# The terms of three field groups: two matrix products a quad instead of three

## What is computed

```python
emb = embed_table[f_ix, x_idx]
lin1 = w1_table[f_ix, x_idx].sum(axis=1, keepdims=True) + w1_bias
s = emb.sum(axis=1)
fm = 0.5 * ((s * s).sum(-1) - (emb * emb).sum(axis=(1, 2)))[:, None]
h = emb.reshape(n, F * D)
h = relu(h @ mlp_w1 + mlp_b1)
h = relu(h @ mlp_w2 + mlp_b2)
mlp_out = h @ mlp_w3 + mlp_b3
x0 = emb.transpose(0, 2, 1)
last = x0
feats = []
for W in (cin_w0, cin_w1, cin_w2):
    last = einsum('ndl,ndf,klf->ndk', last, x0, W)
    feats.append(last)
cin_result = concatenate(feats, -1).sum(axis=1) @ lin_w + lin_b
return lin1 + fm + mlp_out + cin_result
```

## Time and profile before

| what | value |
|---|---|
| time, median of 3 (lowest, highest) | 494.3 us (493.42, 496.37) |
| the profiled execution: time, span | 494.42 us, 492.6 us |
| mean granted clock of PE | 0.989 |
| PE, DVE, ACT, POOL busy | 455.9, 413.2, 369.8, 343.7 us |
| gathers | 358, from 3.6 us to 454.8 us |
| first `main` of tile 0 | 63.22 us |

### The profile page before, as it was taken

The page is one execution under the profiler, slowest core; times in us unless marked ns, Lnnn a source line. Parts: engine busy times, 40 slices in busy tenths (PEclk is TensorE's granted clock), DMA queues, the critical chain, the costliest instruction groups (busy, mean ns, idle before and its releaser), DMA issues.

```text
span 492.6 us, 6838 instructions
## 1 busy us (share of the span) xinstructions
PE 455.9 (93%) x2179; PEld 385.8 (78%) x2179; DVE 413.2 (84%) x873; ACT 369.8 (75%) x726; POOL 343.7 (70%) x363
## 2 busy tenths in 40 slices
PE   0998986899999999999999999999999999999698
PEld 0995764788888888888888788888888888878476
DVE  6163369789999999999999999899999999989756
ACT  0163496488888888888888888888898888788684
POOL 5777777777777777777777777777777777777000
PEclk9999999799999999999999999999999999999989
DMA  8953695222222222222222222122222222222000
GB/s 164 216 159 29 110 205 146 7 8 9 7 8 8 7 9 7 9 8 9 7 8 7 8 8 8 7 8 8 8 8 8 7 9 7 8 8 9 1 0 2
DMA packets 21602, 15.64 MB, mean 32 GB/s; under 512 B 12786, under 2 KB 19903, under 8 KB 21439
## 3 DMA queue, kind: packets, MB, share of 16 engines
q0 software_dynamic: 11456, 3.14, 18.4%
q1 hardware_dynamic: 7106, 10.05, 8.4%
q10 hardware_dynamic: 3005, 2.01, 2.0%
HBM read 14.97 MB, written 0.21 MB: 31 GB/s over the span
## 4 chain that ended last, share of the span: by engine, by line
POOL 65%; issue 21%; PE 5%; ACT 5%; DVE 1%; DMA 1%; POOLq 0%; DVEq 0%
POOL emb L506 65%; ACT ps_s L605 2%; ACT z_hi L598 2%; PE ps_mlp L1152 1%; ACT z_hi L600 1%; PE ps_q L1107 1%; PE ps_y L1138 1%; PE ps_s L1094 1%; PE ps_q L1108 0%; PE ps_q L1109 0%; DVE z_lo L804 0%; DMA emb<-rows,idx_raw 0%; DMA idx_raw<-x_idx 0%; PE ps_y L1194 0%; PE ps_y L1193 0%
## 5 line engine op out<-in xcount | busy, mean ns | idle before, releaser
L506 POOL DMA_INDIRECT emb<-rows,idx_raw x358 | 343.3, 959 | 111.4 <-issue 108.9
L804 DVE TENSOR_TENSOR z_lo<-ps_s,z_hi 128x512 fp32r<-128x512 f32 (+1 forms) x192 | 131.1, 683 | 35.0 <-ACT ps_s L605 34.4
L598 ACT ACTIVATE z_hi<-ps_s 128x512 fp32r<-128x512 f32 (+1 forms) x192 | 114.1, 594 | 37.5 <-PE ps_s L1094 37.1
L605 ACT ACTIVATE ps_s<-ps_s 128x512 f32<-128x512 f32 (+1 forms) x192 | 113.3, 590 | 0.7
L1107 PE MATMUL ps_q<-z_lo,zw_hi 128*127 128x512 f32 (+1 forms) x192 | 79.6, 415 | 8.0 <-DVE z_lo L804 4.8
L1193 PE MATMUL ps_y<-look_hi,one_hot 128*128 128x442 f32 x232 | 85.0, 366 | 0.6 <-issue 0.4
L1094 PE MATMUL ps_s<-xt,pick 128*128 128x512 f32 (+1 forms) x192 | 77.1, 404 | 5.4 <-ACT x_two L591 4.9
L1194 PE MATMUL ps_y<-look_lo,one_hot 128*128 128x442 f32 x232 | 82.2, 356 | 0.0
L1109 PE MATMUL ps_q<-z_hi,zw_hi 128*127 128x512 f32 (+1 forms) x192 | 76.0, 396 | 0.0
L1108 PE MATMUL ps_q<-z_hi,zw_lo 128*127 128x512 f32 (+1 forms) x192 | 76.0, 396 | 0.0
L1107 PEld LDWEIGHTS ps_q<-z_lo,zw_hi 128*127 128x127 f32 (+1 forms) x192 | 36.5, 190 | 20.9 <-issue 11.0
(11 more groups left out here) (187 smaller groups left out, 686.7 us busy)
## 6 DMA issues: line engine op xcount, KB each, us to landing
emb<-rows,idx_raw POOLq DMA_INDIRECT x358, 3.0
w_space<-rows SPq DMA_DIRECT2D x2, 728.9 KB
m_space<-rows SPq DMA_DIRECT2D x2, 728.9 KB
w_space<-key_scratch SPq DMA_DIRECT2D x1, 1408.0 KB, 7.8
w<-cin_w SPq DMA_DIRECT2D x2, 416.0 KB, 5.9
w<-cin_w ACTq DMA_DIRECT2D x2, 416.0 KB, 9.0
w_space<-cin_w SPq DMA_DIRECT2D x2, 416.0 KB, 8.5
w_space<-cin_w ACTq DMA_DIRECT2D x2, 416.0 KB, 8.2
```

The costliest lines, as they stand in the source:

```text
L506: pool.indirect_dma_start(emb[t % EMB][:, f, :], None, rows, bass.IndirectOffsetOnAxis(row_ix[:, t, f:f + 1], 0)).then_inc(gathered[t] if ...
L598: act.activation(z_hi[0:k, c, :], ps[0:k, :], ACT.Square)
L605: act.activation(ps[0:k, :], ps[0:k, :], ACT.Square).then_inc(hi_ready, 1)
L804: z = dve.tensor_tensor(z_lo[0:k, u % NC, :], ps, z_hi[0:k, u % NC, :].bitcast(F32), ALU.subtract)
```

## The change

The three-group terms get by with two products a quad. One matrix `zt` holds both parts of the weights at different rows of the chunk. A triple (a, b, c) can be reached from the pair (a, c) with field b, or from the pair (b, c) with field a. The high part of its weight stands at the pair (a, c) and field b; the low part at the pair (b, c) and field a. Where the fields are 9, 16 and 17, the low part stands at the same pair, and at a second place of the field. For that `xt` now holds 30 places instead of 26: RUN = 10 fields from each of 0, 8 and 16 on (SHIFT = 8, RUNS = 3), so that fields 8, 9, 16 and 17 stand twice. `zt` is then multiplied by the low and by the high squares: two products.

With it go: `copy_by_position` copies 480 elements a partition, not 416; `copy_last_early` has four pieces (160, 160, 32 and 64 elements), not two (288 and 64); the third chunk's copy has 32 rows, not 26; `mlp_w1` comes by six DMAs on SP instead of two, `t_moved` by four instead of two, and the setup's chain to `zt` is longer (a PE transpose and a mask instead of one ACT copy; three ACT copies and three DVE instructions instead of one each; the product that makes the linear rows reads `zt` and so waits for the last of these).

Two places in the hand-written order change as well: ACT's `copy_last_early` stands after `square(14, 11)`, not before it, and DVE's `hidden2(14)` stands before `z_low(15, 0)`, not after it.

```diff
 GROUPS = (9, 9, 8)
+RUN, SHIFT, RUNS = 10, 8, 3
...
-        zt_hi = sb("zt_hi", [P, 3 * STEP + P], F32R)
-        zt_lo = sb("zt_lo", [P, 3 * STEP + P], F32R)
+        zt = sb("zt", [P, LIN + P], F32R)
...
                     by_step = mlp_w1.rearrange("(c e k) h -> e k c h", e=2, k=F)
                     for e in range(2):
-                        sp.dma_start(m1_raw[STEP * e:STEP * e + F, :, :], by_step[e]).then_inc(m1_in, 16)
+                        for f0, f1 in RANGES:
+                            r = STEP * e + place_of(f0)
+                            sp.dma_start(m1_raw[r:r + f1 - f0, :, :], by_step[e, f0:f1]).then_inc(m1_in, 16)
...
-            sp.dma_start(t_moved[:, 0, :], bass.AP(yl_dram.tensor, yl_dram.offset + F2 * W + X12,
-                                                   [[N3, N1], [W, N2], [1, N3]])).then_inc(t_in, 16)
-            sp.dma_start(t_moved[:, 1, :], bass.AP(yl_dram.tensor, yl_dram.offset + X12 + X13,
-                                                   [[W, N1], [N3, N2], [1, N3]])).then_inc(t_in, 16)
+            for rs, cs, term, row, offset, steps in (
+                    (ROWS_AC, slice(F2, F3), 0, 0, NX_ + O23, [[W, N1], [N2, N3], [1, N2]]),
...
+                sp.dma_start(t_moved[rs, term, cs],
+                             bass.AP(yl_dram.tensor, yl_dram.offset + row * W + offset, steps)).then_inc(t_in, 16)
...
             def copy_last_early():
...
-                for fs in (slice(0, EARLY), slice(F - LOOKS, F)):
-                    act.activation(by_pos[:, :, fs], emb[(T - 1) % EMB][:, fs, 0:D].rearrange("p f d -> p d f"), ACT.Copy)
+                for c0, c1 in ((0, RUN), (RUN, 2 * RUN), (2 * RUN, EARLY_AT), (LATE_AT, ONE)):
+                    fs = slice(field_at(c0), field_at(c0) + c1 - c0)
+                    act.activation(by_pos[:, :, c0:c1], emb[(T - 1) % EMB][:, fs, 0:D].rearrange("p f d -> p d f"),
+                                   ACT.Copy)
...
-                act.activation(by_pos[:, :, 0:F], emb[t % EMB][:, :, 0:D].rearrange("p f d -> p d f"),
+                rows_t = emb[t % EMB][:]
+                act.activation(by_pos[:, :, 0:ONE].rearrange("p d (g c) -> p d g c", c=RUN),
+                               bass.AP(rows_t.tensor, rows_t.offset,
+                                       [list(rows_t.ap)[0], [1, D], [SHIFT * R, RUNS], [R, RUN]]),
                                ACT.Copy).then_inc(by_pos_ready, 2)
...
                     if u == NU - 2 and t + 1 < T - 1:
                         copy_by_position(t + 1)
+                    square(t, u)
                     if u == NU - 1 and t + 1 == T - 1:
                         copy_last_early()
-                    square(t, u)
-                    if u == NU - 1 and t + 1 == T - 1:
                         copy_last_late()
...
                 x_low(t, 0)
                 x_low(t, 1)
+                hidden2(t - 1)
                 z_low(t, 0)
-                hidden2(t - 1)
                 add_third(t - 1)
...
-                    pe.matmul(ps_t[:], zt_hi[:, w], lo_x, start=(q == 0), stop=False)
-                    pe.matmul(ps_t[:], zt_lo[:, w], hi_x, start=False, stop=False)
-                    mt = pe.matmul(ps_t[:], zt_hi[:, w], hi_x, start=False, stop=(q == NQ - 1))
+                    pe.matmul(ps_t[:], zt[:, w], lo_x, start=(q == 0), stop=False)
+                    mt = pe.matmul(ps_t[:], zt[:, w], hi_x, start=False, stop=(q == NQ - 1))
```

More of the change, by code:

```diff
@@ L40, with place_of, field_at @@
 SHARES = 4
+def place_of(f):
+    return f + (RUN - SHIFT) * (0 if f < RUN else 1 if f < SHIFT + RUN else 2)
+def field_at(c):
+    return SHIFT * (c // RUN) + c % RUN
 def look_tables():
@@ L45, in look_tables, with pair_tables @@
     return rows.astype(np.float32), np.broadcast_to(np.arange(WIDE, dtype=np.float32), (P, WIDE))
-def pair_tables(f_all, step, low, lin_row):
+def pair_tables(step, low, lin_row):
     first = [sum(GROUPS[:g]) for g in range(3)]
     within = [(first[g] + i, first[g] + j) for g in range(3) for i in range(GROUPS[g]) for j in range(i, GROUPS[g])]
-    cross = [(first[g] + i, first[h] + j) for g, h in ((0, 1), (0, 2), (1, 2))
+    cross = [(first[g] + i, first[h] + j) for g, h in ((0, 2), (1, 2), (0, 1))
              for i in range(GROUPS[g]) for j in range(GROUPS[h])]
@@ L55, in pair_tables @@
     place = {p: n for n, p in enumerate(within)}
-    columns = within + [None, cross[-1]] + cross[:-1] + [(x,) for x in range(f_all)]
+    one = RUNS * RUN
+    pairs = [tuple(place_of(x) for x in pair) for pair in within + cross[-1:] + cross[:-1]]
+    columns = pairs[:nw] + [(one,)] + pairs[nw:] + [(c,) for c in range(one)] + [()] * (step - one)
     pick = np.zeros((P, 2, len(columns)), np.float32)
@@ L59, in pair_tables @@
         for c, pair in enumerate(columns):
-            if pair is None:
-                pick[f_all, e, c] = pick[low + f_all, e, c] = 1.0
-            else:
-                for x in pair:
-                    pick[step * e + x, e, c] = 1.0
-                    pick[low + step * e + x, e, c] = 1.0
+            for x in pair:
+                r = x if x == one else step * e + x
+                pick[r, e, c] = 1.0
+                pick[low + r, e, c] = 1.0
     to_sq = np.zeros((P, 3, P), np.float32)
@@ L83, in pair_tables @@
     cross_sq[(len(cross) - 1) % P, 1, P - 1] = 0.5
-    put = np.zeros((P, lin_row + f_all), np.float32)
-    for x in range(f_all):
-        put[x, lin_row + x] = 1.0
+    put = np.zeros((P, lin_row + step), np.float32)
+    for x in range(sum(GROUPS)):
+        put[x, lin_row + place_of(x)] = 1.0
     fm = np.zeros((P, 5), np.float32)
@@ L599, in square @@
                 if c == 2:
-                    act.activation(z_hi[LIN:LIN + F, c, :], ps[LIN:LIN + F, :], ACT.Copy)
+                    act.activation(z_hi[LIN:P, c, :], ps[LIN:P, :], ACT.Copy)
                 if c == 0 and not (t == T - 1 and u == 0):
@@ L669, in _ @@
             act.dma_start(yl_dram, yl).then_inc(y_stored[6], 16)
-            act.activation(t_own[:], ps_y[0:X12, BANK - N3:BANK], ACT.Copy).then_inc(t_copied, 1)
             act.wait_ge(keys_out, 1)
@@ L691, in _ @@
                                scale=0.5).then_inc(zw_hi_ready, 1)
[L692 removed]
+            act.wait_ge(t_step, 3)
             act.wait_ge(const_ready, CONSTS)
[L694 to L695 removed]
+            for f0, f1 in T_HIGH:
+                c = LIN + place_of(f0)
+                act.activation(zt[:, c:c + f1 - f0], t_sum[:, f0:f1], ACT.Copy, scale=0.5)
+            act.activation(t_high[:], t_sum[:, 0:N1], ACT.Copy, scale=0.5).then_inc(zt_hi_ready, 1)
             act.wait_ge(zlin_done, 1)
[L697 removed]
+            act.activation(zw_hi[LIN:P, 2, 0:NW], ps_q[0][LIN:P, 0:NW], ACT.Copy).then_inc(zw_hi_ready, 1)
             square(0, 0)
@@ L1222, in _ @@
             pe.wait_ge(by_row_copied, 6)
-            pe.wait_ge(t_step, 2)
-            zlin = ps_q[0][0:LIN + F, 0:NW]
+            pe.wait_ge(zt_lo_ready, 1)
+            zlin = ps_q[0][:, 0:NW]
             pe.matmul(zlin, put[0:F, :], by_row[0:F, 3, 0:NW], start=True, stop=False)
-            pe.matmul(zlin, t_pad[:], cross_sq[0:X12, 0, 0:NW], start=False, stop=True).then_inc(zlin_done, 1)
+            for n in range(2):
+                mm = pe.matmul(zlin, zt[:, 0:P].bitcast(F32), cross_sq[:, 0, 0:NW], start=False, stop=(n == 1))
+            mm.then_inc(zlin_done, 1)
             za = ps_t[:, 0:NROW]
```

131 lines of the change are left out of this document (75 added, 56 removed).

## The result

The changed kernel takes 502.56 us (median of 4 executions, 498.74 to 503.13), the kernel before 493.95 in the same comparison: a ratio of 1.0133, with a 95% interval of 1.0103 to 1.0164 (the two medians alone stand further apart, 8.6 us or 1.7%). The forecast was 490.6. The profiled execution took 502.31 us with a span of 500.5, 7.9 more than before.

A forecast was written before the change was run, and what follows sets the result against it. The gathers were taken to hold the kernel up to tile 14's copy, the engines behind it. From the profiled 494.42 us, -0.83, -2.79 and -0.23 made -3.85: 490.6 us, with an 8-in-10 range of 489.3 to 493.0.

The forecast's parts named there:

- What bounds the kernel: POOL's gathers hold tile 14's copy at 430.49 us; the engines hold what comes behind it, tiles 14 and 15.
- rival 1: PE is the bound and all 14.7 us of removed products come back, giving 479.7 us; chance 0.03.
- The tail: Behind tile 14's copy: -0.83 us at x_all(15), then -2.79 at square(15, 2) and -0.23 at the end.
- The wait's second cost: After PE's 2.75 us wait in tile 15 the clock halves, so eight products take 2.13 us, not 1.46.
- The longer copy: Copying 480 elements instead of 416 costs ACT +0.12 us by the rows' slope; only tile 14's copy counts.
- A tile: Up to tile 13, a quarter of 0.92 us saved: 25.85 us a tile instead of 26.09, ending in ACT's wait.
- The setup: Before tile 0: +2.0 us, bounds 0 and 4, hidden by the gathers with 2.25 us to spare at tile 14.
- The loads of `mlp_w1`: In the setup, four more SP issues at 0.50 us ahead of cin_w1's second half: 0.5 us, range 0 to +2.0.
- `t_moved` and the chain to `zt`: In the setup: two more t_moved issues, about 1.0 us, and extra ACT and DVE steps to the linear rows, 0.5.
- Rival 2: A half-clock stretch stays or appears, looked for at tile 14's wait: up to +1.8 us, 490.6 to 492.4; chance 0.14.
- Rival 4: Slower because t_moved delays the setup, deciding at 8.6 us later; at 11 us the time is 499; chance 0.05.
- rival 3: Tiles get no faster and a setup 2.0 to 4.0 us late reaches the end: 491.2 to 493.2 us; chance 0.10.

The follow-up runs named there:

- e4: The kernel before without one of the three three-group products (high squares by low weights) in all 64 quads; 494.56 us, ratio 0.9984.
- e3: The kernel before with only the change's two reordered steps, ACT's copies for tile 15 and DVE's hidden2(14); 491.11 us, ratio 0.9917.
- e7: The kernel before with only DVE's hidden2(14) moved ahead of z_low(15, 0); 491.25 us, ratio 0.9930.
- e11: The kernel before plus PE's transpose of the 26x26 block of yl, its result unread; 495.15 us, ratio 1.0006 without its two longest executions.
- e1: The kernel before with mlp_w1 loaded by six DMAs instead of two, in the same place; 498.57 us, ratio 1.0072.
- e5: The changed kernel with cin_w1 and cin_w0 loaded ahead of mlp_w1, dependent ACT and DVE work moved; 494.35 us, ratio 1.0007 to the kernel before.

## Why the prediction was wrong

**What bounds the kernel** was half right. PE is not the bound: e4's missing products change next to nothing, and rival 1 is out. That the gathers are it holds for the one trace that was read, where ACT waits 1.35 us ahead of tile 14's copy. In e3, e4 and e7, with the same setup and the same tiles but for e4's product, that copy starts at nearly the same time, 430.17 to 430.55, but with no wait: tile 2's came 1.0 to 1.5 us later than in the earlier trace rows, and twelve tiles of 26.09 bring it there. So the kernel stood on the edge between the gathers and DVE's pace, and the time to spare was 1.4 us in one execution and nothing in three others.

**The tail** was right by its steps: 0.94 us saved up to `x_all(15)` against 0.83 summed, 2.96 from there to the end against 3.02. The wait's second cost, the fall of the clock behind it (0.67 of these 3.02), is luck of the execution, though: e11's trace has the same wait of 2.75 us, no fall, and `picked` 1.56 us behind the start of the eight products, where the earlier trace rows have 2.13:

```profile
468.46 1.73 PE L1155 MATMUL ps_mlp<-m_hi,xt 128*128 128x400 f32 x8 [2.75 <-DVE by_row L863]
```

Of the smaller terms, the four pieces take 1.10 us to the late one, as worked out. The longer copy costs 0.03 us (0.98 against 0.95), not 0.12; the 0.05 from the Trainium skill's "ScalarE: Activation LUTs", "What ACT_TABLE_LOAD costs", that I set aside for the rows' slope, was nearer. The difference of two copies of unlike shape was no slope.

**A tile** gains 0.03 us, not the quarter of 0.92 that I took, because DVE's 24.57 us do not change. With 26.06 a tile the margin for a late setup was at most the 1.35 us of the earlier trace rows, and not the 4.25 (2.0 for the setup and 2.25 to spare) of the sum.

**The setup** is the step that failed: "Together +2.0, bounds 0 and 4 ... So it costs nothing". It measured 13.5 us at tile 2's copy, and its bounds didn't hold it. By its terms:
- The loads of `mlp_w1`, 0.5 with a bound of 2.0, are 6.1 us, in the changed kernel's own trace and in e1. I priced the issues, 0.5 us each, and argued that the same bytes move. They move, at 162 instead of 210 GB/s. The issue came 1.7 us later, within the bound; the other 4.4 are the landing, which the sum left out. The earlier trace rows had the warning: PE already waited 1.13 us for `cin_w1`, the load behind them.
- `t_moved` and the chain to `zt`, 1.5, are 2.0 in e5 up to the first `main`, and 3.0 up to tile 2's copy, some of it at the low clock. That term was about right. In the changed kernel's own trace the wait for `t_moved` hides: DVE waits another 4.88 us behind it for ACT, and ACT for the products that run at half clock.
- The clock has no term in my sum of the setup. The products from 58.45 to 68.00 take 9.55 us; in e5, at full clock, the same take 52.21 to 57.59, 5.4. That is 4.2 us. The stretch behind, from ACT's `by_row` to the first `main`, takes 2.2 more than before (68.11 to 76.16 against 57.35 to 63.22); the longer chain and the half clock share these, and the trace does not divide them. Rival 2 had the mechanism, with the place wrong: I looked for it at tile 14.

6.1 + 4.2 + 2.2 make 12.5 of the 13.5; the rest is some 0.5 us in the products ahead of 58.45 and 0.6 in tile 0. With 1.4 spared at tile 14 and 3.9 won in the tail, 13.2 late at tile 13 make 7.9. These are differences of two single executions.

**The rivals.** Rival 4, slower by a late setup, decided at 8.6 us with 0.05, is what happened, by way of the first loads and the clock more than of `t_moved`, whose wait of 2.89 us is real but stands behind the other two. Its margin counts beyond the 2.0 us summed: 13.5 is 11.5 beyond, which by its own sum gives 490.6 + 11.5 - 2.25 = 499.9, and the condition of rival 3, tiles that get no faster, adds 12 x 0.21 = 2.5; together that is the 502 measured. Its chance was too low because the term's bounds were too narrow: they came from issue times, while the row that PE waited for a load gave no upper end at all.
